# Feed forward as a stream of groups, one normalization of all queries, idle products on TensorE, and the input x loaded first

## The reference

```python
def layernorm(x, g=1, b=0): return (x - mean(x)) / sqrt(var(x) + 1e-5) * g + b     # over 128 features
# layer 0, cross block; xn = layernorm(x)
y = layernorm(xn + prob_sparse_self_attention(xn), ln1_g, ln1_b)
o = cross_attention(y, context) @ out_w.T + out_b                                  # 16 heads
z = layernorm(y + o, ln2_g, ln2_b)
h = gelu(z @ ffn_w1.T + ffn_b1)                                                     # 512 hidden units
x = x + layernorm(z + h @ ffn_w2.T + ffn_b2, ln3_g, ln3_b)
x = x + linear_attention(layernorm(x))
x = x + mixture_of_8_experts(layernorm(x))
# layer 1
x = x + cross_attention(layernorm(x), context)                                      # 16 heads of 64, scores as x @ (Wq' Wk) @ context'
x = x + rotary_attention(layernorm(x))
x = x + mixture_of_8_experts(layernorm(x))
```

## Time and profile before

| | |
|---|---|
| median of the runs | 3600.09 us |
| profiled execution | 3611.44 us, span 3609.6 us, mean granted clock 0.94 |
| PE busy | 3310.2 us (92%) |
| DVE, ACT, POOL busy | 2414.8, 1942.3, 1586.5 us (67, 54, 44%) |
| x readable by DVE | 16.14 us after the start |
| feed forward | 1105.3 to 1221.8 us |
| queries 1 | 1444.1 to 1481.4 us |
| cross attention 1 | from 1482.3 us to about 3103 us |

### The profile page before, as it was taken

One profiled execution on the slowest core, in us unless ns is written; L12 is line 12 of the kernel. 1 busy time (PEld: TensorE's weight loads), 2 busy tenths in 40 slices (PEclk: granted clock), 3 DMA queues, 4 the chain that ended last, 5 costly groups with the idle time before them and its releaser, 6 DMA issues. The chain is left out here.

```text
span 3609.6 us, 67171 instructions
## 1 busy us (share of the span) xinstructions
PE 3310.2 (92%) x26109; PEld 1922.9 (53%) x26235; DVE 2414.8 (67%) x5544; ACT 1942.3 (54%) x2669; POOL 1586.5 (44%) x1235
## 2 busy tenths in 40 slices
PE   6789999999995679599999999999999998979998
PEld 3456666666663467354555454555455554655555
DVE  6757777777774443477777777777777775563333
ACT  4446666566664322566666666666666664532222
POOL 4333333333330000277777777777777776210000
PEclk7679999999997769699999999999999998979999
DMA  1033333333320000210111111101111100010000
GB/s 56 20 70 75 75 75 79 72 74 75 83 52 1 1 24 1 70 37 20 37 37 37 37 37 37 37 22 34 37 37 37 37 28 1 1 74 1 1 1 12
DMA packets 90493, 139.18 MB, mean 39 GB/s; under 512 B 14464, under 2 KB 67776, under 8 KB 89408
## 3 DMA queue, kind: packets, MB, share of 16 engines
q1 hardware_dynamic: 90176, 134.87, 13.8%
HBM read 94.41 MB, written 1.05 MB: 26 GB/s over the span
## 5 line engine op out<-in xcount | busy, mean ns | idle before, releaser
L2120 ACT ACTIVATE arena<-banks,arena 128x512 f32<-128x512 f32 x832 | 560.9, 687 | 477.5 <-PE banks L1913 476.6
L1938 PE MATMUL banks<-arena 128*128 128x512 f32 x1664 | 804.5, 603 | 3.0 <-ACT arena L2127 3.0
L1872 POOL TENSOR_TENSOR arena<-arena 128x1024 f32<-128x1024 f32 x256 | 604.0, 2359 | 166.8 <-ACT arena L2127 165.7
L1119 DVE TENSOR_REDUCE arena<-banks 128x1 f32<-128x512 f32 (+1 forms) x896 | 529.8, 628 | 189.5 <-PE banks L1004 184.3
L2022 DVE TENSOR_TENSOR banks<-arena,banks 128x512 f32<-128x512 f32 x640 | 444.6, 695 | 242.8 <-ACT arena L2120 222.9
L1216 ACT ACTIVATE arena<-banks 128x1024 f32<-128x1024 f32 (+1 forms) x448 | 425.1, 964 | 317.0 <-PE banks L1025 314.1
L2039 DVE TENSOR_TENSOR arena<-arena,banks 128x1024 f32<-128x1024 f32 (+1 forms) x448 | 507.5, 1134 | 1.5 <-PE banks L1928 1.0
L2127 ACT ACTIVATE arena<-arena 128x1024 f32<-128x1024 f32 (+1 forms) x448 | 443.0, 989 | 11.6 <-DVE arena L2039 11.4
L1938 PEld LDWEIGHTS banks<-arena 128*128 128x128 f32 x1664 | 290.0, 190 | 223.1 <-issue 202.8
L1913 PE MATMUL banks<-arena 128*128 128x512 bf16 x831 | 314.7, 379 | 2.6
L1912 PE MATMUL banks<-arena 128*128 128x512 bf16 x785 | 298.8, 381 | 4.3 <-issue 0.2
(11 more groups left out here) (345 smaller groups left out, 5218.6 us busy)
## 6 DMA issues: line engine op xcount, KB each, us to landing
arena<-in_ctxT SPq DMA_DIRECT2D x64, 800.5 KB, 5.6
arena<-arena SPq DMA_DIRECT2D x768, 50.0 KB, 2.2
arena<-in_ctx SPq DMA_DIRECT2D x32, 768.0 KB
arena<-in_m2w SPq DMA_DIRECT2D x3, 2048.0 KB, 12.0
arena<-in_xw SPq DMA_DIRECT2D x1, 2048.0 KB, 7.4
weights<-in_weights SPq DMA_DIRECT2D x1, 1918.0 KB, 7.4
arena<-in_ctx SPq DMA_DIRECT2D x32, 32.5 KB
arena<-in_m1w SPq DMA_DIRECT2D x1, 1024.0 KB, 6.2
```

Source lines behind the costliest of these rows:

```text
L1119: eng.tensor_reduce(o, s, AX, ALU.max).then_inc(a_max, 1)
L1872: eng.tensor_tensor(part, part, tiles, ALU.add).then_inc(sums, 1)
L1938: eng.matmul(c.ps[:, R_MIX + v % 2, :], ctxn[:, b, kt * D:(kt + 1) * D], st[:, v % 2, kt, :], start=kt == 0, stop=kt == KT - 1).then_inc(m ...
L2120: eng.activation(st[:, v % 2, kt, :], c.ps[:, n % SB, :], ACT.Identity, bias=hide[:, kt, v // 2:v // 2 + 1])\
```

## The change

1. Setup: SP issues x, consts, rows, weights, in this order, with semaphores of their own (`c.x_loaded`, `c.c_loaded`, `c.loaded`). DVE waits for x alone before the statistics, TensorE and ACT for consts, and all for rows and weights only further on. Four rows of parameters go out of `rows` and four columns into `weights`.
2. `feed_forward` is written anew: buffers for two groups, PSUM banks in four pairs, and each engine's order interleaves groups. Biases and the scale of the second normalization are applied by ACT on turned data, where they are one value for each partition; the residuals enter through identity products. POOL makes the roots by `pow`; ACT has no Ln and Exp in the stage.
3. `queries_1` normalizes all 16 tiles by `Norms` (DVE and POOL), into `c.y`; TensorE turns them in one go after the folding products, and ACT copies one group of 512 columns at a time.
4. `stir`: TensorE products of constants into a bank that nobody reads: 24 at the start of `queries_1`, and in `cross_attention_1` 14 before the mask is turned, 5 after each of four sets of queries, 8 before the first maxima are turned, 10 after the first shift.

```diff
     def sp(eng):
+        eng.dma_start(c.x[:], A["x"].rearrange("(i b) l d -> (b l) i d", b=2)).then_inc(c.x_loaded, 16)
+        eng.dma_start(c.c[:], A["consts"]).then_inc(c.c_loaded, 16)
+        eng.dma_start(c.r[:], A["rows"]).then_inc(c.loaded, 16)
         eng.dma_start(c.w[:], A["weights"]).then_inc(c.loaded, 16)
-        eng.dma_start(c.r[:], A["rows"]).then_inc(c.loaded, 16)
-        eng.dma_start(c.c[:], A["consts"]).then_inc(c.loaded, 16)
-        eng.dma_start(c.x[:], A["x"].rearrange("(i b) l d -> (b l) i d", b=2)).then_inc(c.loaded, 16)
-    m.after = [(c.loaded, 64), (constant, 5)]
+    m.after = [(constant, 5)]
+def stir(c, eng, bank, n):
+    busy = c.C("twice").bitcast(BF16)
+    for _ in range(n):
+        eng.matmul(c.ps[:, bank, :], busy[:, 0:P], busy, start=True, stop=True, skip_group_check=True)
...
 def self_attention(c):
     def dve(eng):
+        eng.wait_ge(c.x_loaded, 16)
         norms.dve_stats(eng, lambda i: c.x[:, i, :])
         for g in range(GROUPS):
             norms.dve_apply(eng, g, lambda i: c.x[:, i, :], lambda i: xn[:, i, :])
+        eng.wait_ge(c.c_loaded, 16)
+        eng.wait_ge(c.loaded, 32)
...
 def feed_forward(c):
     def pe(eng):
+        def proj(g):
+            eng.wait_ge(s["o_copied"], g + 1)
+            eng.wait_ge(s["y_copied"], g + 1)
+            wait_if(eng, s["normed2"], G * (g - 1))
...
+        def hidden(g, f):
+            if f == 0:
+                eng.wait_ge(s["x2T"], g + 1)
+            wait_if(eng, s["hidden"], g * FU + f - 1)
+            eng.matmul(c.ps[:, HIDDEN + f % 2, :], c.W("ffn1", f * P, (f + 1) * P), x2T[:, g % 2, :], start=True,
+                       stop=True).then_inc(s["hidden_psum"], 1)
+        def results(g):
+            eng.wait_ge(s["x2Tb"], g + 1)
+            eng.wait_ge(s["hidden"], (g + 1) * FU)
+            wait_if(eng, s["centred"], G * (g - 1))
+            for j in range(G):
+                w = slice(j * P, (j + 1) * P)
+                eng.matmul(pair(OUT + g % 2, j), x2Tb[:, g % 2, w], c.C("ident"), start=True, stop=False)
+                for f in range(FU):
+                    mm = eng.matmul(pair(OUT + g % 2, j), hT[:, g % 2, f, w], c.W("ffn2", f * D, (f + 1) * D), start=False,
+                                    stop=f == FU - 1)
+            mm.then_inc(s["out_psum"], 1)
+        proj(0)
+        proj(1)
+        turn(0)
+        for g in range(GROUPS):
+            hidden(g, 0)
+            hidden(g, 1)
+            if g + 2 < GROUPS:
+                proj(g + 2)
+            hidden(g, 2)
+            hidden(g, 3)
+            if g + 1 < GROUPS:
+                turn(g + 1)
+            results(g)
     def act(eng):
+        inputs(0)
+        inputs(1)
+        turned(0)
+        for g in range(GROUPS):
+            gelu(g, 0)
+            if g + 2 < GROUPS:
+                inputs(g + 2)
+            for f in range(1, FU):
+                gelu(g, f)
+            if g + 1 < GROUPS:
+                turned(g + 1)
     def dve(eng):
+        for g in range(2):
+            measure(2, g, PROJ, "proj", st2, mv2)
+            norm2(g)
+        for g in range(GROUPS):
+            if g + 2 < GROUPS:
+                measure(2, g + 2, PROJ, "proj", st2, mv2)
+                norm2(g + 2)
+            measure(3, g, OUT, "out_psum", st3, mv3)
+            norm3(g)
...
 def queries_1(c):
     def pe(eng):
+        stir(c, eng, 0, 24)
         eng.wait_ge(s["w_loaded"], 16)
...
         for g in range(GROUPS):
-            turn.pe(eng, g, rows(xn), lambda j: c.ps[:, 2 * j, 0:P], pre.ready)
+            for j in range(G):
+                i = g * G + j
+                eng.wait_ge(norms.ready, i + 1)
+                mm = eng.transpose(c.ps[:, g, j * P:(j + 1) * P], xn[:, i, :], c.C("ident"))
+            mm.then_inc(s["turned"], 1)
...
+    def pool(eng):
+        norms.pool(eng)
     def dve(eng):
-        for g in range(GROUPS):
-            pre.dve(eng, g, lambda j: c.x[:, g * G + j, :], rows(xn), wait=lambda j: wait_if(eng, turn.ready, g * G))
+        norms.dve_stats(eng, lambda i: c.x[:, i, :])
+        for g in range(GROUPS):
+            norms.dve_apply(eng, g, lambda i: c.x[:, i, :], lambda i: xn[:, i, :])
...
 def cross_attention_1(c):
+        stir(c, eng, R_MIX + 1, 14)
         eng.wait_ge(hidden, 3)
...
         for x in range(4):
             queries(0, x)
+            stir(c, eng, R_MIX + 1, 5)
         eng.wait_ge(unit_made, 1)
         for n in range(LEAD):
             scores(n)
             if n == KT + 1:
+                stir(c, eng, R_MIX + 1, 8)
                 turn_peaks(0)
         spread_shift(0)
+        stir(c, eng, R_MIX + 1, 10)
```

More of the change, by code:

```diff
@@ L1281, in act @@
-    def act(eng):
-        for g in range(GROUPS):
-            wait_if(eng, s["x_ready"], g * G)
-            for j in range(G):
-                eng.activation(oT[:, j, :], c.o[:, g * G + j, :], ACT.Identity,
-                               bias=c.W("c_bv")).then_inc(s["o_copied"], 1)
-            ln2.act(eng, g)
-            turn.act(eng, g, B_, lambda j: x2T[:, j * P:(j + 1) * P])
-            for f in range(F0 // P):
-                eng.wait_ge(s["hidden_psum"], g * (F0 // P) + f + 1)
-                eng.activation(hT[:, f, :], c.ps[:, f, :], ACT.Gelu, bias=c.W("ffn_b1", f, f + 1)).then_inc(s["hidden"], 1)
-            ln3.act(eng, g)
@@ L1312, in feed_forward @@
-    m.engines = dict(pe=pe, dve=dve, act=act)
+    FU = F0 // P
+    oT, yT = k.f32(2, G * P), k.f32(2, G * P)
+    n2 = k.f32(2, G, D)
+    x2T, x2Tb = k.f32(2, G * P), k.f32(2, G * P)
+    hT = k.f32(2, FU, G * P)
+    xb, t = k.f32(2, G, D), k.f32(2, G, D)
+    b2 = k.f32(1)
+    st2, mv2, var2, rstd2 = k.f32(2, G, 6), k.f32(2, G, 2), k.f32(2, G), k.f32(2, G)
+    st3, mv3, var3, rstd3 = k.f32(2, G, 6), k.f32(2, G, 2), k.f32(2, G), k.f32(2, G)
+    s = {n: c.sem(f"ff_{n}") for n in (
+        "o_copied", "y_copied", "b2_made", "proj", "stats2", "mean_var2", "var2", "rstd2", "normed2", "turned", "x2T", "x2Tb",
+        "hidden_psum", "hidden", "out_psum", "stats3", "mean_var3", "var3", "rstd3", "centred", "x_biased", "x_ready")}
@@ L1313, in feed_forward @@
+    m.engines = dict(pe=pe, dve=dve, act=act, pool=pool)
     m.after = [(s["x_ready"], PAIRS)]
@@ L1733, in queries_1 @@
     w = k.f32(4, HP * D)
-    xn = k.f32(G, D)
-    pre, turn = Norm(c, k, "q1_pre"), Turn(c, "q1_xT")
-    s = {n: c.sem(f"q1_{n}") for n in ("w_loaded", "fold_psum", "folded")}
+    xn = c.y
+    norms = Norms(c, k, "q1_pre")
+    s = {n: c.sem(f"q1_{n}") for n in ("w_loaded", "fold_psum", "folded", "turned", "xT")}
     def sp(eng):
```

146 lines of the change are left out of this document (98 added, 48 removed).

## The result

The changed kernel takes 3510.66 us (median of 4 runs, 3507.46 to 3513.68), the kernel before 3601.53 beside it: ratio 0.9747, 95% interval 0.9730 to 0.9764, 90.9 us less. The forecast was 97.7 us less, 3502 us, with a range of 3489 to 3530.

A forecast was written before the change was run, and what follows sets the result against it. TensorE bounds both cross attentions, which the change leaves alone, so only short stages gain: setup 11.8, feed forward 59.5, queries 1 20.1, lead of cross attention 1 6.3, together 97.7. From 3600.1 that gives 3502 us, range 3489 to 3530.

The forecast's parts named there:

- Rival 3: Cross attention 0 stays at the low clock after self attention's earlier start: 3620 us, chance 0.02.
- Setup, 11.8 forecast: At the start, x loads first, so normalization starts at 11.0 instead of 22.8 us: 11.8 saved.
- my other end (8.1): At the start, the latest landing of x, taken from the weights' load: 8.1 us, leaving 9.9 saved.
- Rival 4: At the start, x lands with the other loads, so 11.8 saved become 0 to 3: 3512 us, chance 0.05.
- which the projection on TensorE (1.9 us) covers: In feed forward, TensorE's projection hides ACT's copying for group g+2 (1.3 us) between two Gelus.
- The 3 us that I allowed for the low clock: In feed forward, added because TensorE stands still some 3 us ahead of the first hidden product: 57 instead of 54.
- the signs that I had named: Feed forward 57 us, PE share near 0.9, clock 1.00 after 15 us; against: 75 or more, or constants at 0.50.
- Rival 1: Feed forward's stream loses the high clock or waits at each turn: 17 to 33 us more, 3533 taken, chance 0.12.
- Queries 1, 20.1 forecast: Norms and 24 constants run under the weights' load, folding at the high clock: end at 1461.3 instead of 1481.4.
- The first part: Lead of cross attention 1: constants bring the high clock, each set of queries takes 1.04 us less; 4.3 in all.
- rival 2's small form: Constants miss the high clock only in cross attention 1's first 4 us: 14 products take 5.1, not 3.0; 3504 us.
- The second part: Cross attention 1: ten constants hold the clock for the first mixing products, TensorE being the bound: 2.0 us back.

The follow-up runs named there:

- the execution with turned tiles: Changed kernel with 20 turned 128x128 f32 identity tiles in place of the 24 constant products in queries 1: 3514.44 us.
- queries 1 alone: Kernel before with only the new queries 1 (all norms first, one copy a group), without the 24 constants: 3588.21 us, ratio 0.9952.
- ACT reordered: Changed kernel with ACT's feed forward copies for group 2 ahead of group 0's turned copies, group 3's behind the first four Gelus: 3505.39 us, ratio 0.9731.
- early tables: ACT reordered, plus one-column Gelu and Exp activations placed in ACT's waits in feed forward and linear attention: 3504.02 us, ratio 0.9722.
- x in four pieces: Early tables kernel with x loaded in one piece per group, and three more constants behind the turned mask in cross attention 1: 3502.76 us, ratio 0.9716.
- three parts alone: Kernel before with one part each: x loaded first (3591.55 us), feed forward's stream (3549.71), queries 1 without the 24 constants (3588.21).

## Why the prediction was right, and where its terms were off

**The bound.** Right: the two cross attentions have the work and the clock of before, and 91.4 of the 101.1 us between the two profiles are in the four short stretches. Rival 3 fell with it: cross attention 0 took 932.5 to 935.0 us in every kernel but the two profiles of before.

**Setup, 11.8 forecast, 10.8 measured.** The mechanism is right: POOL's root is early, and rows and weights cost nothing on the path (DVE waited 0.50 us for the weights, forecast up to 0.3). x was there 1.2 us later than I worked out from the store of the same size, and still ahead of my other end (8.1); consts landed at about 9.6, not 8.5 to 9, still ahead of the first turning. Rival 4 fell.

**Feed forward, 59.5 forecast, 55.1 to 56.5 measured** (115.1 or 116.5 less 60.0). The prologue is right to 0.1 us: the first hidden product came 10.7 us behind the start, forecast 10.8. The step that failed is "which the projection on TensorE (1.9 us) covers". The projection for group g+2 can't cover the copying for group g+2, since it waits for it: both stood in one line behind the first Gelu. TensorE waited 1.95 us there and 1.19 at the next group, and behind the first wait the clock was low for 4 us. Taking the copies out of that place gave 5.0 us back. The same code in the execution with turned tiles took 57.9: it had the same two waits, and its clock stayed at 1.00 behind the first. So by that one execution about 2.1 of the 5.0 are the clock and 2.9 the waits.

The 3 us that I allowed for the low clock were about right in size, but not safe in place. In the six executions of this code the clock fell behind the wait of 1.95 us three times, ahead of the first hidden products, where I had put it, twice, and once at neither place. The waits that I had argued away came on top. Of the signs that I had named, TensorE's share behind the first 15 us came out (37.7 of 41 us), the clock of 1.00 there did not. Rival 1, the stage at the low clock, was right only for 3 to 4 us at the beginning and 4 behind the wait.

**Queries 1, 20.1 forecast, 21.1 measured.** The 24 constants did hold the clock, 3.6 us of it; without them the stage would have given 17.3 (16.4 measured alone). The excess of 1.0 is in two places: the folding with its copies took 5.9 us (1374.79 to 1380.65), forecast 6.4, and the turning with its copies 2.8, forecast 3.3 with the step between the two.

**Lead of cross attention 1, 6.3 forecast, 3.2 measured, and 0.6 in the body.** The forecast has two parts, 4.3 up to the first mixing product and 2.0 behind it.

The first part was mis-sized: 3.2. The idle products bring the clock up, but the first set ended and the constants behind it ran at 0.50 to 0.67, which cost 1.7 us; three more products gave them back, and then the lead is 4.9 us shorter than before. A clock of 0.50 while constants run was one of the signs that I had named for being wrong. It is rival 2's small form, at another place than I put it. A smaller part is that a set of queries also goes through ACT and DVE, and the sets came nowhere closer than 2.57 us, where I had reckoned with 2.45.

The second part came for another reason than I gave. The first mixing products did run at 1.00, but they do so without the constants too. And of the 1.7 us that they gain at once 0.9 are left after 14 us and 0.3 at the last mixing product: behind them TensorE waits now and then (it is busy 7.37 of 8 us from 1431 to 1439), so it isn't the bound all the time, as I had taken it to be.

By the Trainium skill, "TensorE: Matmul & The Clock Gate", "Part 4: PE-mode transpose", turned tiles don't count as TensorE being busy in the same way as products. The fall at 1391, behind 13 thin turned tiles, fits that, and so does its going when three products stand behind them; but those also fill a wait of 0.75 us, and the experiment with turned tiles didn't tell the two apart, so no run here shows which it was. What I took from this case's own trace in support is weaker than I thought: the 16 turned tiles of linear attention were not unbroken work. They start 0.26 us apart, at DVE's pace, where turned tiles that wait for nothing start 0.21 apart at the low clock (queries 1 alone) and 0.12 at the high one.

**The sum.** 10.8 + 55.4 + 21.1 + 3.8 = 91.1 by the stages (against both profiles of before) and 90.9 by the medians. Of the 6.6 missing, feed forward has 4.1, the lead 2.5 and setup 1.0, less the 1.0 of queries 1. Part of feed forward's is mine in another way: I worked from one profiled execution that was over 10 us above the median, 1.3 of them in that stage, and took the whole difference as a constant. Luck has a small part in the total: queries 1 gave 1.0 more than forecast against the other misses, and the first mixing products had the high clock without my doing.

**The version that beats both, by its median,** is the one with ACT reordered, early tables, x in four pieces and three more constants: 3502.76, ratio 0.9716 against 0.9747; the intervals overlap a little (0.9737 and 0.9730). Its four stages are 7.8 us shorter than the changed kernel's, and linear attention with mixture 0 is 1.0 shorter; in the profiled execution self attention, cross attention 0 and the body were 4.1 longer. The kernels with ACT reordered alone (3505.39) and with the early tables (3504.02) aren't told apart from it by their times.

## What to carry to other kernels

When you write that a transfer or a copy "is covered" by work on another engine, check that this work doesn't itself wait for it; the copy for the next round has to stand ahead of the place where the consumer is free, not behind the last result of this round. A single wait of 2 us on TensorE can cost twice, once for itself and once for the low clock behind it, though not in every execution. Edits of 1 to 5 us are read from the length of their stage in several profiles, since whole times of one kernel spread over 3 to 17 us. A kernel split into stages between barriers lets parts be summed: here three parts alone gave 84.3 of 90.9, and the stages of the fourth most of the rest.

## What the runs showed of the hardware

The granted clock stayed at 0.50 for tens of us while TensorE had work almost without a pause: in self attention of the changed kernel (many small products) 29.1 of 30 us were busy, by durations that include the drain:

```profile
50.00:80.00 30.00, 29.10 (x247) 19.24 (x240) 29.39 (x260) 19.49 (x21) 10.68 (x6) 0.50 0.01 2
```

Busy time is therefore not enough to forecast the clock. Nor is the length of one wait. In queries 1 behind the same 24 constants a wait of 2.21 us left it at 1.00, and one of 3.85 us was followed by 0.50; but behind the wait of 2.98 us ahead of the first mixing product it was 0.50 in the kernel before and 1.00 in the kernel without idle products, and behind the wait of 1.95 us in feed forward 0.50 in the changed kernel and 1.00 in the one with turned tiles. A DMA of x in rows of 512 bytes took 6.5 us to land where the one that stores it took 5.1, and SP needed 2.05 us for the issue behind it; in four pieces the median was 3.9, the four issues took 2.09 us together and the one behind them 0.51. A table load of 1.28 us moves to wherever the first activation of that kind stands, even one of a single column, and the copies behind it need no other (the Gelu's load stood 11.4 us behind the start of feed forward in the changed kernel, behind the copies of the turned tiles, and 6.6 us behind it with the early tables, ahead of them).
